# Causal attention in fp32: the search for row maxima is spread along a concave line, the maxima enter the scores as three bf16 parts, and whole chunks of weights are added on GpSimd

## What is computed

```
t = t + attn(layernorm(t))
q, k, v = split(x @ qkv_w.T + qkv_b)          # 4 heads x 32
att = softmax(where(causal, (q @ k.T) / sqrt(32), -inf))
out = (att @ v) @ out_w.T + out_b
```

## Time and profile before

| | us |
|---|---|
| median of 3 runs | 10961.17 |
| lowest, highest | 10953.19, 10961.48 |
| the profiled execution | 10953.31 |
| its span, first to last instruction | 10951.5 |
| mean granted TensorE clock | 0.940 of full |

### The profile page before, as it was taken

The page is one execution under the profiler, slowest core; times in us unless marked ns, Lnnn a source line. Parts: engine busy times, 40 slices in busy tenths (PEclk is TensorE's granted clock), DMA queues, the critical chain, the costliest instruction groups (busy, mean ns, idle before and its releaser), DMA issues. The chain is left out here.

```text
span 10951.5 us, 166018 instructions
## 1 busy us (share of the span) xinstructions
PE 9227.2 (84%) x59866; PEld 4819.9 (44%) x59866; DVE 7622.5 (70%) x8779; ACT 6061.1 (55%) x12476; POOL 5534.4 (51%) x3721
## 2 busy tenths in 40 slices
PE   7888888888888776677798998988989988799897
PEld 3333333333333333566555555555555554333334
DVE  5999999999999996566556665555665653444633
ACT  4666666767666664111356666666666665233233
POOL 5888889889888885666333323222323320011010
PEclk8999999999999998888889999999999999899898
DMA  2222222222222223666300000000000001200003
GB/s 72 76 77 78 80 78 79 79 78 80 78 80 78 79 77 97 193 195 196 102 2 2 4 5 1 4 1 5 4 1 5 1 10 42 94 1 1 1 1 142
DMA packets 259107, 623.72 MB, mean 57 GB/s; under 512 B 26279, under 2 KB 114447, under 8 KB 255992
## 3 DMA queue, kind: packets, MB, share of 16 engines
q1 hardware_dynamic: 203672, 438.27, 12.2%
q0 software_dynamic: 51840, 169.91, 5.2%
q10 hardware_dynamic: 2784, 4.92, 0.1%
HBM read 572.09 MB, written 40.90 MB: 56 GB/s over the span
## 5 line engine op out<-in xcount | busy, mean ns | idle before, releaser
L978 POOL TENSOR_TENSOR a_dBu<-a_du,a_Bs 128x960 f32<-128x960 f32 (+1 forms) x1280 | 2714.5, 2144 | 222.8 <-DVE a_H L750 202.5
L750 DVE TENSOR_TENSOR_SCAN a_H<-a_pA,a_dBu 128x962 f32<-128x962 f32 (+1 forms) x1280 | 2652.6, 2072 | 107.9 <-ACT a_pA L919 54.7
L919 ACT ACTIVATE a_pA<-a_delta,a_al 128x480 f32<-128x480 f32 (+1 forms) x2560 | 1624.8, 639 | 1148.8 <-DVE a_H L750 1143.9
L541 PE MATMUL a_pY<-a_H,cst 128*128 128x480 f32 (+1 forms) x5120 | 2213.5, 554 | 34.4 <-ACT a_Y L936 34.1
L758 DVE TENSOR_TENSOR a_H<-a_H,a_pC 128x960 f32<-128x960 f32 (+1 forms) x1280 | 1393.8, 1089 | 84.3 <-PE a_pC L541 83.0
L541 PEld LDWEIGHTS a_pY<-a_H,cst 128*128 128x128 f32 x5120 | 976.3, 193 | 707.0 <-issue 541.3
L541 PE MATMUL a_pC<-a_stk,a_sel 96*128 96x480 bf16 (+1 forms) x1280 | 471.6, 368 | 512.3 <-DVE a_H L758 504.1
L3398 POOL TENSOR_TENSOR e_P<-e_P 128x1024 f32<-128x1024 f32 (+1 forms) x80 | 151.8, 1918 | 1437.8 <-ACT e_P L3374 1437.8
L1089 POOL DMA_INDIRECT b_gath<-b_tab,b_idx x648 | 613.5, 947 | 392.1 <-issue 176.1
L2459 POOL TENSOR_TENSOR c_KF<-c_KF,c_dg 128x1056 f32<-128x1056 f32 x192 | 386.3, 2013 | 670.7 <-DVE c_MX L2219 670.3
L3374 ACT ACTIVATE e_P<-e_slot 128x1024 f32<-128x1024 f32 (+1 forms) x464 | 347.5, 796 | 657.0 <-PE e_slot L3129 588.5
(11 more groups left out here) (468 smaller groups left out, 18043.8 us busy)
## 6 DMA issues: line engine op xcount, KB each, us to landing
a_Bs<-a_brows SPq DMA_DIRECT2D x512, 480.0 KB
a_Bs<-a_brows SPq DMA_DIRECT2D x128, 384.0 KB
d_W<-in_d_w SPq DMA_DIRECT2D x32, 1024.0 KB, 7.5
f_W<-in_f_w SPq DMA_DIRECT2D x32, 1024.0 KB, 7.8
b_tab<-b_TT SPq DMA_DIRECT2D x32, 576.0 KB
b_gath<-b_tab,b_idx POOLq DMA_INDIRECT x648
a_zt<-a_sz SPq DMA_DIRECT2D x36, 256.0 KB
a_sz<-a_zt SPq DMA_DIRECT2D x16, 480.0 KB
```

The costliest lines, as they stand in the source:

```text
L541: return pe.matmul(out, lhsT, rhs, start=start, stop=stop, skip_group_check=True)
L750: v.tensor_tensor_scan(span(H[:, g % NH, :], g), factors(g), span(dBu[:, g % ND, :], g), 0.0, ALU.mult, ALU.add).then_inc(S(kind), 1)
L919: s.activation(pA[:, k, at:at + z], delta[:, u % 2, h, 0:z], ACT.Exp, scale=al[:, o + 2 * d, h, n:n + 1]).then_inc(S(kind), 1)
L978: g.tensor_tensor(inner(dBu[:, i % ND, :], i), du[:, u % 2, :, 0:z], Bs[:, p % NB, i % 2, 0:z].unsqueeze(1).broadcast_to([128, 2, z]), ALU ...
```

## The change

The order gets a new line: `others` is also held back, to at most SLACK items beyond the due number of the tile reached, and the due numbers follow the concave hull over the points by which each block's `neg` must be done (score columns of its start less EARLY, items up to it). Layer norm and QKV of the next batch move from blocks 1 to 3 to blocks 3 and 4. The maximum is split in DVE into bf16 high, middle and low parts in three neighbouring columns; the transposes and the adding to the scores become bf16 matmuls, which sum the three parts over the 32 rows of a head. `fold` adds all four tiles of a chunk in three steps, and the chunk is summed once. COST follows. NR, slots and buffers of P stay.

```diff
-    NT, QB, NP, NR, SLACK = L // 128, 512, 12, 4, 2
+    NT, QB, NP, NR, SLACK, EARLY = L // 128, 512, 12, 4, 2, 1024
...
-    ones = ph.sb("ones", [128, 128])
+    ones = ph.sb("ones", [128, 32])
+    onesh = ph.sb("onesh", [128, 128], BF16)
+    identh = ph.sb("identh", [128, 128], BF16)
...
+    most4 = ph.sb("most4", [128, 2, 4])
+    peak = ph.sb("peak", [128, NR, 4, 128], BF16)
+    neg = ph.sb("neg", [128, NR, QB], BF16)
...
-            "most": ("PE", .5), "most_out": ("DVE", 1.07), "peak": ("DVE", .2), "neg": ("PE", .6), "neg_out": ("ACT", .6),
-            "score": ("PE", 1.8), "masked": ("DVE", .43), "exp": ("ACT", 1.02), "av": ("PE", .9), "fold": ("POOL", 4.7),
+            "most": ("PE", .5), "most_out": ("DVE", 1.07), "peak": ("DVE", 1.0), "neg": ("PE", .4), "neg_out": ("ACT", .6),
+            "score": ("PE", 1.8), "masked": ("DVE", .43), "exp": ("ACT", 1.02), "av": ("PE", .9), "fold": ("POOL", 4.8),
...
+        reached[0] = due(n, t)
...
-        while done[0] < due(n, t) and not stuck[0]:
+        while done[0] < reached[0] - SLACK and not stuck[0]:
...
-        put("score", n, t, us=spread(1.7, z))
+        put("score", n, t, us=spread(1.1, z))
...
+    def folded(n, q):
+        groups.append((n, 4 * q + 3))
+        if len(groups) > 2:
+            yield from until("sum", *groups[-3])
+        for t in range(4 * q + 1, 4 * q + 4):
+            for hp in range(2):
+                yield from until("exp", n, t, hp)
+            put("fold", n, t)
+            yield
+        put("sum", n, 4 * q + 3, us=.95)
...
+            while done[0] > reached[0] + SLACK:
+                yield
...
-        if b + 1 < B and 1 <= j < 4:
-            ahead += [(kind, b + 1, g) for g in range(2 * j - 2, min(2 * j, 5)) for kind in ("ln", "qk", "v")]
+        if b + 1 < B and j >= 3:
+            ahead += [(kind, b + 1, g) for g in ((0, 1, 2), (3, 4))[j - 3] for kind in ("ln", "qk", "v")]
...
-    def paired(j, t):
-        return t < 4 * j and t % 4 < 2
+    def folds(j, t):
+        return t < 4 * j
...
+    opened = [plan.index(("neg", n)) + 1 for n in range(1, len(blocks))]
+    corners = [(max(work[tile_no[n, 0]] - EARLY, 0), rest[k]) for n, k in enumerate(opened, 1)]
+    path, at = [(0, 0)], (0, 0)
+    while at[1] < rest[-1]:
+        at = max((p for p in corners if p[1] > at[1]), key=lambda p: ((p[1] - at[1]) / max(p[0] - at[0], 1), p[1]))
+        path.append(at)
+
     def due(n, t):
-        share = work[tile_no[n, t]] / work[-1] * rest[-1]
-        return max(sum(x <= share for x in rest) - 1 - SLACK, 0)
+        share = np.interp(work[tile_no[n, t]], [x for x, _ in path], [y for _, y in path])
+        return max(sum(x <= share for x in rest) - 1, 0)
...
-                        m = pe.transpose(sl[:, 0, k * 128:(k + 1) * 128], peak[:, n % NR, k, :], K["ident"])
+                        m = mm(sl[:, 0, k * 128:(k + 1) * 128], peak[:, n % NR, k, :], identh[:, :])
...
-                        m = mm(sl[h // 2][:, h % 2, 0:z - q0], ones[hs, :], neg[hs, n % NR, q0:z], False, True)
+                        m = mm(sl[h // 2][:, h % 2, 0:z - q0], onesh[hs, :], neg[hs, n % NR, q0:z], False, True)
...
-                    if paired(j, t):
-                        f = upto("fold", n, t) - 1
-                        pe.wait_ge(S("fold"), 2 * f + 2)
+                    if folds(j, t):
+                        f = group_at.index((n, t - 2))
+                        pe.wait_ge(S("fold"), 2 * upto("fold", n, t))
                     for h in range(4):
-                        rhs = P2[:, f % 2, h // 2, h % 2, 0:z] if paired(j, t) else P[:, pbuf(n, t, h // 2), h % 2, 0:z - q0]
-                        m = mm(pZ[32 * h:32 * h + 32, q0:z], ones[:, 0:32], rhs, (n, t) == sum_first[n],
+                        rhs = P2[:, f % 2, h // 2, h % 2, 0:z] if folds(j, t) else P[:, pbuf(n, t, h // 2), h % 2, 0:z - q0]
+                        m = mm(pZ[32 * h:32 * h + 32, q0:z], ones[:, :], rhs, (n, t) == sum_first[n],
                                (n, t) == sum_last[n])
...
+            v.memset(onesh[:, :], 1.0).then_inc(S("ones"), 1)
+            v.tensor_copy(identh[:, :], K["ident"]).then_inc(S("ones"), 1)
...
-                    v.tensor_reduce(peak[:, n % NR, i - 4 * j, 0:128:32], part[:, n % NR, i - 4 * j, :, 0:i // 4 + 1],
-                                    AX.X, ALU.max).then_inc(S(kind), 1)
+                    k = upto(kind, n, i)
+                    most = most4[:, k % 2, :]
+                    high, mid, low = (peak[:, n % NR, i - 4 * j, p:128:32] for p in range(3))
+                    v.tensor_reduce(most, part[:, n % NR, i - 4 * j, :, 0:i // 4 + 1], AX.X, ALU.max).then_inc(S("peak_most"), 1)
+                    v.wait_ge(S("peak_most"), k)
+                    v.tensor_copy(high, most).then_inc(S("peak_high"), 1)
+                    v.wait_ge(S("peak_high"), k)
+                    v.tensor_tensor(mid, most, high, ALU.subtract).then_inc(S("peak_rest"), 1)
+                    v.tensor_tensor(most, most, high, ALU.subtract).then_inc(S("peak_rest"), 1)
+                    v.wait_ge(S("peak_rest"), 2 * k)
+                    v.tensor_tensor(low, most, mid, ALU.subtract).then_inc(S(kind), 1)
...
-                    f = upto(kind, *key) - 1
+                    f = group_at.index((n, t // 4 * 4 + 1))
                     g.wait_ge(S("exp"), max(exps(n, t - 1), exps(n, t)))
-                    if f >= 2:
-                        g.wait_ge(S("sum"), upto("sum", *fold_at[f - 2]))
+                    if t % 4 == 1:
+                        if f >= 2:
+                            n0, t0 = group_at[f - 2]
+                            g.wait_ge(S("sum"), upto("sum", n0, t0 + 2))
+                    else:
+                        g.wait_ge(S("fold"), 2 * upto("fold", n, t - 1))
                     for hp in range(2):
-                        g.tensor_tensor(P2[:, f % 2, hp, :, 0:z], P[:, pbuf(n, t - 1, hp), :, 0:z],
-                                        P[:, pbuf(n, t, hp), :, 0:z], ALU.add).then_inc(S("fold"), 1)
+                        so_far = P[:, pbuf(n, t - 1, hp), :, 0:z] if t % 4 == 1 else P2[:, f % 2, hp, :, 0:z]
+                        g.tensor_tensor(P2[:, f % 2, hp, :, 0:z], so_far, P[:, pbuf(n, t, hp), :, 0:z],
+                                        ALU.add).then_inc(S("fold"), 1)
```

More of the change, by code:

```diff
@@ L2843, in attention @@
     part = ph.sb("part", [128, NR, 4, 4, 5])
-    peak = ph.sb("peak", [128, NR, 4, 128])
-    neg = ph.sb("neg", [128, NR, QB])
+    most4 = ph.sb("most4", [128, 2, 4])
+    peak = ph.sb("peak", [128, NR, 4, 128], BF16)
+    neg = ph.sb("neg", [128, NR, QB], BF16)
     rec = ph.sb("rec", [128, 2, QB])
@@ L2908, in scores @@
             yield from until("av", n0, t0)
-            if paired(blocks[n0][1], t0):
-                yield from until("fold", n0, t0 // 4 * 4 + 1)
+            if folds(blocks[n0][1], t0):
+                yield from until("fold", n0, t0 + (t0 % 4 == 0))
             else:
                 yield from until("sum", n0, t0)
-        while done[0] < due(n, t) and not stuck[0]:
+        while done[0] < reached[0] - SLACK and not stuck[0]:
             yield
@@ L2954, in outputs @@
                 yield
-                if not paired(j, t):
+                if not folds(j, t):
                     put("sum", n, t, us=spread(.85, z))
@@ L2958, in outputs @@
                 elif t % 4 == 1:
-                    spawn(folded(n, t))
+                    spawn(folded(n, t // 4))
             for t in range(tiles(j)[-1] + 1):
-                if paired(j, t):
-                    if t % 4 == 1:
-                        yield from until("sum", n, t)
-                else:
+                if t % 4 == 3 or not folds(j, t):
                     yield from until("sum", n, t)
@@ L2969, in outputs @@
             yield
[L2971 to L2979, removed]
+    groups = []
+    def folded(n, q):
[8 more added lines that the diff above has]
+        put("sum", n, 4 * q + 3, us=.95)
     def normed(b, g):
@@ L3091, in attention @@
         plan += todo + [("neg", n)]
-    done, stuck = [0], [False]
+    done, reached, stuck = [0], [0], [False]
     tile_at = [(n, t) for n, (b, j) in enumerate(blocks) for t in range(tiles(j)[-1] + 1)]
     tile_no = {key: k for k, key in enumerate(tile_at)}
-    def paired(j, t):
-        return t < 4 * j and t % 4 < 2
+    def folds(j, t):
+        return t < 4 * j
     WEIGHT = {"ln": 3.0, "qk": 2.0, "v": 1.0, "neg": 1.0}
@@ L3111, in attention @@
     sum_last = [next(k for k in sums[::-1] if k[0] == n) for n in range(len(blocks))]
-    fold_at = [key for kind, key in ph.order if kind == "fold"]
+    group_at = [(n, t) for n, t in (key for kind, key in ph.order if kind == "fold") if t % 4 == 1]
     def group(b, g):
@@ L3136, in _ @@
             pe.wait_ge(S("load"), 32)
-            pe.wait_ge(S("ones"), 1)
+            pe.wait_ge(S("ones"), 3)
             mm(pO[:, 0:2], w[:, 384:512], w[:, 514:516]).then_inc(S("bias_mm"), 1)
@@ L3369, in _ @@
```

(4 more changed lines are left out.)

## The result

The changed kernel takes 10853.26 us in the median of 4 runs (10838.21 to 10865.90), the kernel before 10961.33 beside it: ratio 0.990, 95% interval 0.9888 to 0.9913. That is 108 us less, where 228 less was forecast, and 3 us above the range. The profiled execution has a span of 10846.5 us; phase e went from 1298.6 to 1194.9 us, all else from 9652.9 to 9651.6.

A forecast was written before the change was run, and what follows sets the result against it. PE was taken to bound phase e, so work it is spared comes off nearly one for one. 130 + 63 + 5 + 45 - 20 = 223 us less put the profiled execution at 10730 us, median 10733 us, range 10665 to 10850.

The forecast's parts named there:

- Term 4: Phase e's search bursts: with the new order the clock should stay up beside the search, 45 us less (bounds 0 to 85).
- Term 2: Sums of 40 whole chunks in phase e: one sum each instead of three, 63 us less, at most 71.
- Terms 1 and 3: Phase e on PE: maxima added in bf16, 130 us less, priced from phase c's row; transposes in bf16, 5 us less.
- Term 5: Making `peak` on DVE: one reduction becomes five operations, some subtractions waiting for POOL; 20 us more on PE's time.
- the cover is 40% of idle time: DVE in phase e: busy about 650 of some 1075 us, its idle share covering the added `peak` operations.
- half of 37 reach PE: Subtractions for `peak` waiting for POOL: 37 us more on DVE, half let through to PE, taken as 20 us.
- Term 6: POOL's folds: 80 instructions become 240, 460 us instead of 152, covered while search runs; 5 us at the end taken as nothing.
- Rival B: Late fold: each wide chunk makes PE wait one fold, 113 us in all, total 10846 us; chance 0.11.
- Idle time left at 116 us: PE in phase e: slots freed sooner but search wants them at the same time, so idle time was left unchanged.
- A: Phase e's search bursts stay at half clock because slots don't allow both; no pace gain, total 10778 us; chance 0.15.
- C: Shared interface: every `peak` meets a whole POOL instruction and PE feels it all, 169 instead of 20 us, 10882; chance 0.07.
- D: Slower: thinner PE work lets the clock fall over all of phase e; 11203 us with half the work at 1.2 GHz; chance 0.04.

The follow-up runs named there:

- pace_high: Kernel before plus the new line and only the high bf16 part of each maximum, old pair folds kept: ratio 0.9856, phase e 1147.1 us.
- old_pace: Changed kernel with the old straight line, no hold and QKV in its old blocks; bf16 maxima and chunk folds kept: ratio 0.9977, phase e 1271.4 us.
- pace_only: Kernel before with the new line alone (hold, hull, QKV moved), fp32 maxima and pair folds kept: ratio 0.9947, phase e 1241.8 us.
- high_only: Changed kernel with only the high bf16 part of each maximum, cast and three subtractions removed: ratio 0.9842, phase e 1125.6 us.
- half_exp: Changed kernel with the exponential over half of each tile's columns, P first set to ones by a memset: ratio 0.9893, phase e 1181.6 us.

## Why the prediction was wrong, step by step

Put on in the order pace, folds, one bf16 part, split, phase e goes 1298.6, 1241.8, 1188.9, 1125.6, 1194.9. Against the forecast the pace gained 12 us more, while the sums fell short by 10, bf16 by 72 and `peak` by 49. Together that is 119 us, the gap between the 223 us forecast and the 104 measured. How the gain divides between sums and bf16 hangs on their order: with one bf16 part before the folds (pace_high) the phase goes 1241.8, 1147.1, 1125.6.

- **Term 4, pace:** 45 forecast, 57 measured, with 84 us left at 1.2 GHz. Right by itself; the changed kernel does not keep it, since it is back at 236 us.
- **Term 2, fewer sums:** 63 forecast. The two widths lost 62.6 us of busy time, as priced; the phase fell by 53 when the folds came first and by 22 when they came after the bf16 part.
- **Terms 1 and 3, bf16:** 135 forecast. The busy time fell by 117 and 5 us, so the row of phase c was a fair price (84 us against 97.9). But the phase fell by 63 (idle time rose by 26 us and time at 1.2 GHz by 48), or by 95 where bf16 came first. In either order terms 1 to 3 gave 116 of the 198 us forecast. The step that failed is the first paragraph's "what PE is spared comes off the time, nearly one for one": with 162 us less of PE busy time (1142 to 980) idle time rose from 100 to 146 us, and the time at 1.2 GHz from 84 to 132.
- **Term 5, `peak`:** 20 forecast, 69 measured. DVE's own extra was foreseen (102; the four new groups take 95). What failed is "the cover is 40% of idle time" and "half of 37 reach PE": 0.8 us of the phase went per us of DVE (69 of 85), and the cast waited for POOL too. The price of meeting POOL, 37 us, was close to what the 22 casts (21 us over their 0.18) and 11 subtractions (22 us) lost, but by luck in part: the prediction had subtractions alone, more of them and each for a shorter time. Of the 69, 27 are idle time, the rest busy time at a time when 104 us more run at 1.2 GHz.
- **Term 6, POOL:** 454.5 us busy (460 forecast); PE waited 1.4 us for a fold before a sum. Rival B is out.
- **Idle time left at 116 us:** 173, most of the rise as PE's waits for the search's reductions (41.3 to 90.1 us).
- **Rivals.** What A and C name came in part: C in the place foreseen (DVE behind POOL), for 33 operations, the whole split costing 69 of its 169 us; A by its sign in the clock, but not for its reason, since the pacing works. D's slower kernel did not come. Its mechanism, less work and a lower clock, is what old_pace shows (401 us at 1.2 GHz), and it is in the changed kernel too, which is back at 236 us at 1.2 GHz from pace_only's 84.

Why the time is limited by DVE at 56% busy isn't settled. The runs show how much of the phase a us of each engine's busy time was worth: DVE 0.6 (split, old folds), 0.8 (split, chunk folds) and 0.9 (mask, with the order altered), PE 0.4 (search in bf16) to 0.7 (pace_only to high_only), ACT 0.1. They also show that the planner's estimate for the search matmuls does not matter. That a search slot goes PE, DVE, PE in turn, and that scores take two slots of three, would give such a chain, but it was only argued: no run has another slot. Nor does a run part idle time from the clock: whether waits bring the lower clock, or the thinner work does, stays open.

## What to carry to other kernels

Before taking PE work off one for one, ask what it waits for between its instructions: where PE and DVE hand a few buffers to and fro, DVE's time can count for most of its length at half occupancy, and part of what PE is spared comes back as idle time and as time at the lower clock. Small DVE operations between SBUF tensors must not be priced at their duration if POOL runs long instructions beside them; drop them, shorten POOL's, or let them read PSUM. In the changed kernel 119 of the 288 widest reductions of PSUM slots began beside POOL, and they took 1.22 us like the others. A number that cancels, such as a softmax's shift, needs no exact parts.

## What was not expected of the hardware

A DVE cast, which reads one SBUF tensor, can wait for POOL as well: all 22 casts that made a part of `peak` and began beside POOL lasted until an instruction of POOL ended. In phase c the same kind took 178 to 184 ns throughout, though 59 of its 192 casts of 128x24 began beside POOL; the reduction before the cast (128x4 out) also reads one SBUF tensor, and 23 of 72 began beside POOL without a delay. Which casts wait the runs don't show, and rows 9 could not have warned of it. In half_exp a cast stood beside a memset on POOL (timeline, start, us):

```profile
9245.74 10.34 POOL L3415 MEMSET e_P<- 128x12288 f32 x1 [297.26 <-POOLq L50]
9245.96 10.20 DVE L3255 CAST e_identh<-cst 128x128 bf16<-128x128 f32 x1
```

The cast took 10.20 us instead of the 0.16 of the changed kernel, ending at 9256.16, with the memset's end at 9256.08. The Trainium skill, GPSIMD Engine Reference, section 1, says that POOL's SBUF interfaces are shared with VectorE, with contention for instructions in a 2-port mode or with two SBUF inputs. For two inputs the trace agrees: all 11 first subtractions that began beside POOL waited, 2.2 us on the mean. Whether the casts ran in a 2-port mode no trace here shows.

The other surprise is the clock. Single waits of PE such as the 3.25 us at 9690 stand ahead of whole stretches at 0.50, where PE is then busy for 5.99 of 6.00 us. But a wait isn't needed: at 9478.45 the clock fell after PE had been busy for 3.79 of 4 us (the changed kernel, columns as above).

```profile
9474.40:9478.40 4.00, 3.79 (x16) 0.95 (x14) 3.97 (x5) 0.00 (x0) 0.00 (x0) 1.00 0.00 0
9478.50:9488.50 10.00, 5.96 (x34) 1.81 (x32) 5.45 (x17) 2.07 (x3) 0.00 (x0) 0.50 0.00 1
```
